# A graph layer on one core: the waits for products and for cleared places move from VectorE to TensorE

## Chip, cores and metric

The kernel runs on one core of one Trainium2 chip. The metric is the device time in microseconds (us) of one execution. The engines are named as the profile does: PE is TensorE's matmul, PEld its weight load, DVE VectorE, ACT ScalarE, POOL GpSimd, SP SyncE.

## The reference

x has 50,000 rows (nodes) of 256, and there are 25,000 edges, sorted by their destination `dst`. The parts that matter:

```
msg = relu(relu(layernorm(x))[src] + edge_attr)
p = msg @ W_fc.T + b_fc                      # one row of 256 per edge
scores = p @ Q.T                             # 4 heads
alpha = softmax of scores over the edges of one node, per head
pooled = segment_sum(alpha[:, h] * p, dst)   # per node, per head
gate = softmax(mean of p over the node's edges @ Wg.T + bg)
out = x + sigmoid(sum over h of gate[n, h] * pooled[n, h])
```

Since `gate` and `alpha` are numbers, each edge has one weight in the end, and the result of a node is the sigmoid of a weighted sum of its edges' rows `p`, added to x.

## The kernel before

**Edge stage.** The edges stand in 196 tiles of 128 rows. For each tile the x rows are gathered, normalized, added to the edge rows, transposed and multiplied, and the product p is kept in SBUF (`p_keep`, 124 tiles and 8 more places). 64 tiles are spilled to memory and reloaded later by SP, which raises `p_ready` as the tiles are there. In this stage a table is made as well: for each step of the node stage the address of its tile in `p_keep` and the place of its node tile in PSUM (`path`, twelve words per six steps), and per six steps one word that says how many tiles of p and how many cleared groups it needs (`needs_of`, in the tile `few`).

**Weights.** A stage of small operations, mostly on DVE, makes the weight of each edge.

**Node stage.** The 50,000 nodes are 391 tiles of 128, in 98 groups of four. A step pairs one tile of edges with one tile of nodes that it touches; there are 586. For each step DVE makes `spread` (L1248), a 128x128 matrix that holds an edge's weight in the column of its node, and PE multiplies it with the tile of p and adds the result in PSUM at the node tile's place (L829; in 32-bit floats the matrix makes two passes of it, so a step is two MATMUL and two LDWEIGHTS in the profile). PSUM has twelve places, three slots of a group each. When a group's steps are done (`stepped`), ACT takes the sigmoid of it (L597) and clears the slot (L573), which raises `zeroed`; POOL adds x (L478), and ACT issues the store (L605) and the next load of x (L552, every fourth by POOL at L482). A group is 512 KB in and 512 KB out.

**Order of the node stage.** It runs in turns of twelve steps, two half turns of six each; after the first turn both PE and DVE are in a loop (L836 and its like on DVE). The tile `spread` has twelve slots, and DVE's `spreads` waits for `stepped`, which starts at twelve, so it may make the spreads of six steps when PE has finished the six that used the same slots. In the half turn PE reads its twelve words with one TENSOR_LOAD (L819), waits for `spread_ready` before the first and the fourth step, and issues six matmuls. DVE reads the word of `needs_of` with one TENSOR_LOAD (`need_word`, L1252), waits for `p_ready` (L1256) and for `zeroed` (L1257), then makes six spreads. So PE needs no waits of its own for p and for the cleared places: a spread is made only when both are there. Each such wait compares a semaphore with a register, and loads and register instructions are done by the engine's sequencer, in order.

Of the kernel before, what the change touches and what calls it, by code (L numbers as in the profile page):

```python
# [34 lines left out]
def gnn_layer(nc, x, src, dst, edge_attr, w_fc, b_fc, q_w, g_w, b_g, out):  # L35
# [7 lines left out]
    TILES = -(-E // P)  # L43
# [33 lines left out]
    GROUPS = -(-NODES // GROUP)  # L77
    STEPS = TILES + NODES - 1
    AHEAD = 12
    HALF = AHEAD // 2  # L80
    TURNS = STEPS // AHEAD
# [23 lines left out]
    with ExitStack() as ctx:  # L105
# [3 lines left out]
        def sem(name):  # L109
            return ctx.enter_context(nc.semaphore(name))  # L110
# [37 lines left out]
        needs_of, done_of, free_of = few[0:1, :], few[32:33, :], few[64:65, :]  # L148
# [120 lines left out]
        words_stored, words_in = sem("words_stored"), sem("words_in")  # L269
# [19 lines left out]
        p_ready, zeroed = sem("p_ready"), sem("zeroed")  # L289
# [376 lines left out]
        def _(pe):  # L666
            pe.wait_ge(const_set, 10)
            pe.wait_ge(src_f32, 1)
            for b in range(BLK):
                last = nc.tensor.transpose(bank[:, 6, b * P:(b + 1) * P], src_f[:, b, :], ident[:, :])  # L670
# [3 lines left out]
            for c in range(KD):  # L674
                for t in range(KT):
                    last = nc.tensor.transpose(bank[:, 7, c * T + t * P:c * T + (t + 1) * P],
                                               w_nat[:, t, c * P:(c + 1) * P], ident[:, :])
            last.then_inc(w_turned, 1)
            for t in range(KT):
                last = nc.tensor.transpose(bank[:, 5, t * K:(t + 1) * K], qg[:, t * P:(t + 1) * P],  # L680
                                           ident[0:K, 0:K])
# [3 lines left out]
            for c in range(KD + 1):  # L685
                for t in range(KT):
                    lhs = b_col[:, t:t + 1].broadcast_to([P, P]) if c == KD else w_nat[:, t, c * P:(c + 1) * P]
                    last = nc.tensor.matmul(bank[:, 4, c * K:(c + 1) * K], lhs, q_t[:, t, :],
                                            start=(t == 0), stop=(t == KT - 1))
# [84 lines left out]
            for k in range(K):  # L774
                for b in range(BLK):
                    last = nc.tensor.transpose(bank[:, k // 2, (k % 2) * TP + b * P:(k % 2) * TP + (b + 1) * P],
                                               logits[:, b * P:(b + 1) * P, k], ident[:, :])
# [31 lines left out]
            for n, o, cols in ((7, 2 * P, slice(0, P)), (6, 0, slice(P, STEPS))):  # L809
                for b in range(BLK):  # L810
                    last = nc.tensor.matmul(bank[:, n, o:o + cols.stop - cols.start], c_of(b), sel_1[:, b, cols],
                                            start=(b == 0), stop=(b == BLK - 1))
# [2 lines left out]
            places = bank[:, :, :].rearrange("p b n -> p (b n)")  # L815
            p_rows = p_keep[:, :, :].rearrange("p t d -> p (t d)")

            def steps(half, s0, k0, n, apart=3):
                _, words = nc.values_load_multi_w_load_instructions(  # L819
                    path_of[:, bass.ds(half * WORDS, WORDS)], engines=[mybir.EngineType.PE], min_val=0,  # L820
                    max_val=(RING + STAGE) * T, skip_runtime_bounds_check_because=bound_by_shape)
                for k in range(n):
                    if k % apart == 0:
                        pe.wait_ge(spread_ready, s0 + k0 + min(k + apart, n))
                    p_at = nc.s_assert_within(words[k], 0, (RING + STAGE - 1) * T,
                                              skip_runtime_bounds_check_because=bound_by_shape)
                    place = nc.s_assert_within(words[HALF + k], 0, (POS - 1) * T,
                                               skip_runtime_bounds_check_because=bound_by_shape)
                    nc.tensor.matmul(places[:, bass.ds(place, T)], spread[:, k0 + k, :], p_rows[:, bass.ds(p_at, T)],  # L829
                                     start=False, stop=True, skip_group_check=True).then_inc(stepped, 1)  # L830

            pe.wait_ge(words_in, 64)
            pe.sem_inc(stepped, AHEAD)
            steps(0, 0, 0, HALF, 1)
            steps(1, 0, HALF, HALF)
            with pe.Fori(1, TURNS) as turn:  # L836
                for h in range(2):
                    steps(2 * turn + h, turn * AHEAD, h * HALF, HALF)
            s0 = TURNS * AHEAD
            steps(2 * TURNS, s0, 0, HALF)  # L840
            steps(2 * TURNS + 1, s0, HALF, STEPS - s0 - HALF)

        @block.vector
        def _(dve):
            steps = [0]
# [398 lines left out]
            def spreads(s0, k0, n):  # L1245
                dve.wait_ge(stepped, s0 + k0 + n)
                for k in range(k0, k0 + n):
                    v.tensor_scalar(spread[:, k, :], bank[:, 7, P:2 * P], rel[:, bass.ds(s0 + k, 1)],  # L1248
                                    wgt[:, bass.ds(s0 + k, 1)], ALU.is_equal, ALU.mult).then_inc(spread_ready, 1)

            def need_word(n):
                return dve.value_load(needs_of[:, bass.ds(n, 1)], min_val=257, max_val=(1 << 15) - 1)  # L1252

            def need(n):
                word = need_word(n)
                dve.wait_ge(p_ready, word & 255)  # L1256
                dve.wait_ge(zeroed, word >> 8)  # L1257

            dve.wait_ge(words_in, 64)
            first, second = need_word(0), need_word(1)  # L1260
            dve.wait_ge(p_ready, first & 255)
            dve.wait_ge(zeroed, first >> 8)
            dve.wait_ge(wgt_summed, 1)
            then(v.tensor_copy(wgt[:, 0:P], bank[:, 7, 2 * P:3 * P]))
            dve.sem_inc(wgt_ready, 1)
            spreads(0, 0, HALF)
            dve.wait_ge(p_ready, second & 255)
            dve.wait_ge(zeroed, second >> 8)
            spreads(0, HALF, HALF)
            dve.wait_ge(wgt_summed, 2)  # L1270
            then(v.tensor_copy(wgt[:, P:STEPS], bank[:, 6, 0:STEPS - P]))
            with dve.Fori(1, TURNS) as turn:
                for h in range(2):
                    need(2 * turn + h)
                    spreads(turn * AHEAD, h * HALF, HALF)
            s0 = TURNS * AHEAD
            need(2 * TURNS)
            spreads(s0, 0, HALF)
            dve.wait_ge(p_ready, TILES)
            dve.wait_ge(zeroed, GROUPS)  # L1280
            spreads(s0, HALF, STEPS - s0 - HALF)

            slot = (FULL - 1) % 4
# [35 lines left out]
```

## Time and profile before

| | us |
|---|---|
| median of 3 runs | 739.03 (735.18 to 739.16) |
| profiled execution | 734.6 |
| its span | 732.9 |
| PE, PEld busy | 548.9, 434.1 |
| DVE busy | 487.6 |
| ACT, POOL busy | 383.3, 453.4 |
| node stage | about 401 to 724 |

Register, branch, semaphore and DMA-issuing instructions don't count as busy; in a view of one line they stand under the engine's name with a q (PEldq, DVEq, ACTq), with their own durations. The DMA share is the mean busy share of the core's 16 DMA engines; packets that overlap can bring it a little over 1. The granted clock was 0.946 of full speed in the mean over the span. The waits view says for how long an engine was idle and whose end released it; "issue" means that nothing in the profile released it, so that its own sequencer was late.

### The profile page before, as it was taken

The page shows a single profiled execution, that of the slowest core. Times are in us where ns is not written, and L with a number is a line of the kernel's source. Part 1 is how long each engine was busy: PE and PEld are TensorE (multiplying, and loading weights), DVE is VectorE, ACT ScalarE, POOL GpSimd, SP SyncE. Part 2 cuts the span into 40 slices and gives each one's busy share as a digit, 9 for nine tenths or more (in the row PEclk, how much of TensorE's full clock was granted, in tenths as well). Part 3 has the DMA queues.
Part 4 walks back from the last instruction along what each step waited for, and adds up shares of the span by engine and source line. Part 5 has one row for each costly group of instructions (what it writes and reads, how often), then busy time and mean ns, then how long its engine had stood idle before and what let it go on. Part 6 is the DMA issues. An engine that isn't in the chain of part 4 may idle for free.

```text
span 732.9 us, 12416 instructions
## 1 busy us (share of the span) xinstructions
PE 548.9 (75%) x2474; PEld 434.1 (59%) x2475; DVE 487.6 (67%) x1644; ACT 383.3 (52%) x661; POOL 453.4 (62%) x339
## 2 busy tenths in 40 slices
PE   2417988878779868879403998888888778877785
PEld 2205876666558656758202876776667566665564
DVE  4208678788879768769798766666565655555555
ACT  2105455656457545647211254666666666666674
POOL 7765565665560656550053366777877887778785
PEclk9999899999999999989855999999999999999999
DMA  7434455555553468775300799999999999999999
GB/s 223 131 93 134 147 173 174 165 174 154 174 170 114 129 224 271 237 234 191 115 0 1 247 355 383 314 307 329 357 319 329 325 327 339 325 337 336 341 333 332
DMA packets 137238, 171.53 MB, mean 234 GB/s; under 512 B 10096, under 2 KB 123784, under 8 KB 137202
## 3 DMA queue, kind: packets, MB, share of 16 engines
q10 hardware_dynamic: 91344, 90.23, 37.6%
q1 hardware_dynamic: 33010, 42.70, 18.6%
q0 software_dynamic: 12848, 38.20, 16.5%
q8 instruction: 12, 0.20, 0.1%
q14 instruction: 24, 0.20, 0.1%
HBM read 111.50 MB, written 59.60 MB: 233 GB/s over the span
## 4 chain that ended last, share of the span: by engine, by line
PE 52%; issue 12%; ACT 11%; DVE 10%; another core or an unknown queue 5%; ACTq 4%; DVEq 3%; POOL 2%; DMA 2%; POOLq 0%; SPq 0%
PE bank L745 24%; PE bank L829 18%; PE bank L735 7%; ACT arena L597 5%; DVE spread L1248 3%; ACT bank L573 3%; POOL arena L478 2%; ACTq L600 2%; DVEq L1252 1%; ACT arena L505 1%; ACTq L552 1%; ACTq L605 1%; ACT arena L497 1%; DMA p_keep<-p_spill 1%
## 5 line engine op out<-in xcount | busy, mean ns | idle before, releaser
L829 PE MATMUL bank<-p_keep,spread 128*128 x1172 | 274.1, 388 | 51.6 <-DVE spread L1248 46.7
L829 PEld LDWEIGHTS bank<-p_keep,spread 128*128 128x128 f32 x1172 | 219.0, 192 | 107.5 <-issue 79.8
L1248 DVE TENSOR_SCALAR spread<-bank,rel,wgt 128x128 f32<-128x128 f32 x586 | 195.8, 404 | 128.5 <-PE bank L829 72.8
L478 POOL TENSOR_TENSOR arena<-arena 128x1024 f32<-128x1024 f32 x96 | 224.9, 2352 | 73.1 <-ACT arena L597 72.7
L745 PE MATMUL bank<-w_all,arena 128*128 128x264 f32 (+1 forms) x784 | 228.0, 417 | 53.2 <-ACT arena L505 40.2
L745 PEld LDWEIGHTS bank<-w_all,arena 128*128 128x128 f32 (+1 forms) x784 | 143.7, 204 | 78.9 <-ACT arena L505 50.9
L597 ACT ACTIVATE arena<-bank 128x1024 f32<-128x1024 f32 x97 | 99.2, 1023 | 139.3 <-PE bank L829 120.3
L443 POOL DMA_INDIRECT p_keep<-in_x_dram,idx x124 | 120.8, 975 | 72.6 <-issue 31.5
L505 ACT ACTIVATE arena<-bank 128x256 f32<-128x256 f32 x196 | 73.6, 376 | 124.2 <-PE bank L735 71.0
L443 POOL DMA_INDIRECT arena<-in_x_dram,idx x72 | 70.1, 973 | 64.7 <-ACT arena L497 33.7
L573 ACT ACTIVATE bank<-zero 128x1024 f32<-128x1024 f32 x98 | 100.5, 1026 | 3.0
L735 PE MATMUL bank<-ident,arena 128*128 128x128 f32 x392 | 80.5, 289 | 24.4 <-DVE arena L1061 11.3
L735 PEld LDWEIGHTS bank<-ident,arena 128*128 128x128 f32 x392 | 56.8, 149 | 53.2 <-DVE arena L1061 13.5
L1061 DVE TENSOR_TENSOR arena<-arena 128x256 f32<-128x256 f32 x196 | 79.8, 408 | 6.7 <-issue 3.9
L497 ACT ACTIVATE arena<-p_keep,negmr,rstd 128x256 f32<-128x256 f32 x124 | 73.6, 594 | 20.3 <-issue 14.1
L1075 DVE TENSOR_TENSOR p_keep<-bank,bias 128x512 f32<-128x512 f32 x97 | 66.0, 680 | 0.0
L1073 DVE TENSOR_TENSOR logits<-bank,bias 128x16 f32<-128x16 f32 x97 | 16.5, 170 | 64.7 <-PE bank L745 34.6
L1055 DVE BATCH_NORM_STATS2 stats<-p_keep 128x6 f32<-128x256 f32 x124 | 51.7, 419 | 1.0 <-DMA p_keep<-in_x_dram,idx 0.6
L497 ACT ACTIVATE arena<-arena,negmr,rstd 128x256 f32<-128x256 f32 x72 | 42.7, 593 | 9.5 <-DVE negmr L1099 7.5
L1055 DVE BATCH_NORM_STATS2 stats<-arena 128x6 f32<-128x256 f32 x72 | 30.2, 419 | 0.0
L449 POOL TENSOR_SCALAR arena<-arena 128x1024 f32<-128x1024 f32 x1 | 3.9, 3852 | 42.5 <-DVEq L1183 42.5
L482 POOL DMA_DIRECT2D arena<-in_x_dram x24 | 18.6, 773 | 17.6 <-POOL arena L478 14.8
(202 smaller groups left out, 190.6 us busy)
## 6 DMA issues: line engine op xcount, KB each, us to landing
out_dram<-arena ACTq DMA_DIRECT2D x97, 512.0 KB, 4.5
arena<-in_x_dram ACTq DMA_DIRECT2D x73, 512.0 KB, 5.4
arena<-in_edge_attr_dram SPq DMA_DIRECT2D x48, 512.0 KB
arena<-in_x_dram POOLq DMA_DIRECT2D x24, 512.0 KB, 5.8
p_spill<-p_keep SPq DMA_DIRECT2D x16, 512.0 KB
p_keep<-p_spill SPq DMA_DIRECT2D x16, 512.0 KB, 5.8
p_keep<-in_x_dram,idx POOLq DMA_INDIRECT x124
arena<-in_x_dram,idx POOLq DMA_INDIRECT x72
```

The source lines that it names most:

```text
L443: pool.indirect_dma_start(out=x_row(t), out_offset=None, in_=x, in_offset=bass.IndirectOffsetOnAxis(ap=idx[0:rows_of(t), t:t + 1], axis=0) ...
L478: pool.tensor_tensor(yout[:, slot, :, :], yout[:, slot, :, :], xin[:, slot, :, :], ALU.add).then_inc(summed, 1)
L497: nc.scalar.activation(u[0:n, t % 4, :], x_row(t), ACT.Relu, bias=negmr[0:n, m:m + 1], scale=rstd[0:n, m:m + 1]).then_inc(ln_done, 1)
L505: nc.scalar.activation(msg_t[:, t % 4, :, 0:n], bank[:, TURNS_IN[t % len(TURNS_IN)], 0:D].rearrange("p (c e) -> p c e", c=KD)[:, :, 0:n], ...
L573: nc.scalar.activation(bank[:, 2 * z:2 * z + 2, :], zero[:, 0:1].unsqueeze(2).broadcast_to([P, 2, 512]), ACT.Copy).then_inc(zeroed, 1)
L597: nc.scalar.activation(yout[:, k % YS, :, :], places(k % SLOTS, GROUP), ACT.Sigmoid).then_inc(sig_done, 1)
L735: last = nc.tensor.transpose(bank[:, TURNS_IN[t % len(TURNS_IN)], c * P:c * P + n], u[0:n, t % 4, c * P:(c + 1) * P], ident[0:n, 0:n])
L745: last = nc.tensor.matmul(bank[0:n, 2 + t % 4, 0:NT], msg_t[:, t % 4, c, 0:n], w_all[:, c, :], start=(c == 0), stop=(c == KD - 1))
L829: nc.tensor.matmul(places[:, bass.ds(place, T)], spread[:, k0 + k, :], p_rows[:, bass.ds(p_at, T)], start=False, stop=True, skip_group_che ...
L1055: v.bn_stats(stats[0:n, m, :], x_row(t)).then_inc(stats_done, 1)
L1061: v.tensor_tensor(u[0:n, t % 4, :], u[0:n, t % 4, :], ea[0:n, t % BODY, :], ALU.add).then_inc(added, 1)
L1248: v.tensor_scalar(spread[:, k, :], bank[:, 7, P:2 * P], rel[:, bass.ds(s0 + k, 1)], wgt[:, bass.ds(s0 + k, 1)], ALU.is_equal, ALU.mult).th ...
```

## The change

The two waits for `p_ready` and `zeroed`, and the load of the word that they compare with, leave DVE and go to PE, where they stand after the load of the path words and before the six matmuls. DVE's spreads now wait for `stepped` alone. The last half turn waits for constants.

```
+            def held(half):
+                word = pe.value_load(needs_of[:, bass.ds(half, 1)], min_val=257, max_val=(1 << 15) - 1)
+                pe.wait_ge(p_ready, word & 255)
+                pe.wait_ge(zeroed, word >> 8)
+
+            def held_last():
+                pe.wait_ge(p_ready, TILES)
+                pe.wait_ge(zeroed, GROUPS)
+
-            def steps(half, s0, k0, n, apart=3):
+            def steps(half, s0, k0, n, apart=3, last=False):
                 _, words = nc.values_load_multi_w_load_instructions(
                     path_of[:, bass.ds(half * WORDS, WORDS)], engines=[mybir.EngineType.PE], min_val=0,
                     max_val=(RING + STAGE) * T, skip_runtime_bounds_check_because=bound_by_shape)
+                if last:
+                    held_last()
+                else:
+                    held(half)
                 for k in range(n):
...
-            def need(n):
-                word = need_word(n)
-                dve.wait_ge(p_ready, word & 255)
-                dve.wait_ge(zeroed, word >> 8)
-
-            dve.wait_ge(words_in, 64)
-            first, second = need_word(0), need_word(1)
-            dve.wait_ge(p_ready, first & 255)
-            dve.wait_ge(zeroed, first >> 8)
             dve.wait_ge(wgt_summed, 1)
             then(v.tensor_copy(wgt[:, 0:P], bank[:, 7, 2 * P:3 * P]))
             dve.sem_inc(wgt_ready, 1)
             spreads(0, 0, HALF)
-            dve.wait_ge(p_ready, second & 255)
-            dve.wait_ge(zeroed, second >> 8)
             spreads(0, HALF, HALF)
...
             with dve.Fori(1, TURNS) as turn:
                 for h in range(2):
-                    need(2 * turn + h)
                     spreads(turn * AHEAD, h * HALF, HALF)
             s0 = TURNS * AHEAD
-            need(2 * TURNS)
             spreads(s0, 0, HALF)
-            dve.wait_ge(p_ready, TILES)
-            dve.wait_ge(zeroed, GROUPS)
             spreads(s0, HALF, STEPS - s0 - HALF)
```

On PE, at the head of the first half turn in the loop, this stood before; `path` is the table of twelve words per half turn, ISA and REGISTER_ALU are register instructions:

```order
L819 TENSOR_LOAD path
L824 ISA
L829 ISA [waits spread_ready]
L829 MATMUL bank<-p_keep,spread 128x256
L829 ISA
```

And this stands there now (L828, L837 and L842 are the lines that were L819, L824 and L829; `few` is the tile of the words that say what is needed):

```order
L828 TENSOR_LOAD path
L819 ISA
L819 TENSOR_LOAD few
L819 ISA x2
L820 REGISTER_ALU
L821 REGISTER_ALU [waits p_ready]
L837 ISA [waits zeroed]
L842 ISA [waits spread_ready]
L842 MATMUL bank<-p_keep,spread 128x256
L842 ISA
```

Between the load of the path words and the first matmul there are a second load, three ISA and two REGISTER_ALU instructions more, and the waits for `p_ready` and `zeroed`. The second half turn of the loop has the same.

On DVE, at the head of its loop, before:

```order
L1252 TENSOR_LOAD few
L1252 ISA x2
L1256 REGISTER_ALU
L1257 REGISTER_ALU [waits p_ready]
L1246 ISA [waits zeroed]
L1248 ISA [waits stepped]
L1248 TENSOR_SCALAR spread<-bank,rel,wgt 128x128
```

And now (L1261 was L1248):

```order
L1261 ISA [waits stepped]
L1261 TENSOR_SCALAR spread<-bank,rel,wgt 128x128
L1261 ISA
L1261 TENSOR_SCALAR spread<-bank,rel,wgt 128x128
L1261 ISA
L1261 TENSOR_SCALAR spread<-bank,rel,wgt 128x128
```

The load, its two checks and the two waits are gone, and the six spreads follow one another as before, held by `stepped` alone.

## Rows read from the trace of the kernel before

**Rows 1.** The page, parts 1 and 2: busy time, and the span in 40 slices
```profile
PE 548.9 (75%) x2474; PEld 434.1 (59%) x2475; DVE 487.6 (67%) x1644; ACT 383.3 (52%) x661; POOL 453.4 (62%) x339
...
PEclk9999899999999999989855999999999999999999
DMA  7434455555553468775300799999999999999999
GB/s 223 131 93 134 147 173 174 165 174 154 174 170 114 129 224 271 237 234 191 115 0 1 247 355 383 314 307 329 357 319 329 325 327 339 325 337 336 341 333 332
```

**Rows 2.** Busy time by stretches of the node stage (columns in the first row)
```profile
core 0: us, PE busy (x) PEld busy (x) DVE busy (x) ACT busy (x) POOL busy (x), PEclk, DMA share, GB/s
401.00:419.00 18.00, 18.00 (x85) 15.62 (x84) 14.61 (x44) 4.10 (x4) 4.37 (x3) 1.00 0.63 207
419.00:431.00 12.00, 11.41 (x53) 9.61 (x52) 8.58 (x26) 6.15 (x6) 6.81 (x4) 1.00 0.99 324
431.00:528.00 97.00, 85.71 (x374) 69.13 (x374) 61.60 (x185) 57.27 (x56) 72.23 (x36) 1.00 1.01 341
528.00:724.00 196.00, 156.32 (x654) 122.29 (x653) 109.65 (x328) 127.48 (x125) 157.70 (x79) 0.98 1.02 334
...
470.00:489.00 19.00, 17.59 (x81) 14.83 (x80) 12.10 (x37) 11.47 (x12) 13.53 (x8) 1.00 0.89 282
```

**Rows 3.** The waits from 401 to 729 us, longest first
```profile
engine line waited for: us in total, times, longest us
ACT arena L597 <- PE bank L829: 120.3, 74, 23.9
PEld bank L829 <- issue: 79.4, 72, 3.1
...
DVE spread L1248 <- ACT bank L573: 49.9, 27, 4.5
PE bank L829 <- DVE spread L1248: 46.7, 50, 2.7
```

**Rows 4.** Loads of L819, by stretches: 400-419, 470-489, 419-729, 401-431, 431-528, 528-724
```profile
engine op xcount: duration ns min/median/max, first and last start us, forms
...
L819 PEldq TENSOR_LOAD <-path x7: 848/857/865, 401.3 to 416.8; - x7
...
L819 PEldq TENSOR_LOAD <-path x7: 847/1130/1599, 470.2 to 485.7; - x7
...
L819 PEldq TENSOR_LOAD <-path x90: 846/1749/3016, 419.8 to 722.7; - x90
...
L819 PEldq TENSOR_LOAD <-path x11: 846/858/2638, 401.3 to 427.4; - x11
...
L819 PEldq TENSOR_LOAD <-path x32: 847/1586/2643, 431.6 to 528.0; - x32
...
L819 PEldq TENSOR_LOAD <-path x55: 847/1813/3016, 528.0 to 722.7; - x55
```

**Rows 5.** Loads of L819: from 634 to 639 us, then from 634 to 640.5
```profile
L819 PEldq TENSOR_LOAD <-path x2: 1294/1630/1965, 634.1 to 637.3; - x2
...
L819 PEldq TENSOR_LOAD <-path x3: 1294/1965/2268, 634.1 to 640.1; - x3
```

**Rows 6.** The chain of waits around one register load of ACT (L600)
```profile
642.41 0.03 issue
642.44 0.05 ACTq L600
642.49 0.03 issue
642.52 0.75 ACTq L600
643.27 0.03 issue
643.30 0.15 ACTq L600
643.45 0.03 issue
643.48 0.02 ACTq L600
643.50 0.04 issue
643.54 0.04 ACTq L596
643.58 0.04 issue
643.62 1.03 ACT arena L597
```

**Rows 7.** One-word loads: DVE (L1252) 400-419, 470-489, 419-729; then ACT (L600) 419-729
```profile
L1252 DVEq TENSOR_LOAD <-few x7: 301/310/316, 403.8 to 418.1; - x7
...
L1252 DVEq TENSOR_LOAD <-few x7: 301/315/979, 469.8 to 488.7; - x7
...
L1252 DVEq TENSOR_LOAD <-few x88: 300/578/1474, 420.4 to 717.3; - x88
...
L600 ACTq TENSOR_LOAD <-few x32: 279/766/1646, 423.1 to 724.2; - x32
```

**Rows 8.** Timeline, 396 to 401 us: the start of the node stage
```profile
396.91 4.20 PE L811 MATMUL bank<-logits,arena 128*128 128x128 f32 x8 [19.60 <-DVEq L1243]
...
398.65 0.29 DVE L1264 COPY wgt<-bank 128x128 f32<-128x128 f32 x1 [1.95 <-PE bank L811]
398.66 0.34 PEld L811 LDWEIGHTS bank<-logits,arena 128*128 128x128 f32 x1 [0.43 <-issue]
399.11 2.00 DVE L1248 TENSOR_SCALAR spread<-bank,rel,wgt 128x128 f32<-128x128 f32 x6 [0.16 <-DVE wgt L1264]
```

More of the change, by code:

```diff
@@ L840, in _ @@
             steps(2 * TURNS, s0, 0, HALF)
-            steps(2 * TURNS + 1, s0, HALF, STEPS - s0 - HALF)
+            steps(2 * TURNS + 1, s0, HALF, STEPS - s0 - HALF, last=True)
         @block.vector
@@ L1249, in spreads @@
                                     wgt[:, bass.ds(s0 + k, 1)], ALU.is_equal, ALU.mult).then_inc(spread_ready, 1)
-            def need_word(n):
-                return dve.value_load(needs_of[:, bass.ds(n, 1)], min_val=257, max_val=(1 << 15) - 1)
-            def need(n):
-                word = need_word(n)
-                dve.wait_ge(p_ready, word & 255)
-                dve.wait_ge(zeroed, word >> 8)
-            dve.wait_ge(words_in, 64)
-            first, second = need_word(0), need_word(1)
-            dve.wait_ge(p_ready, first & 255)
-            dve.wait_ge(zeroed, first >> 8)
             dve.wait_ge(wgt_summed, 1)
```

## Prediction, made before the changed kernel was run

> **What bounds the kernel now.** I read the page's parts 1 and 2 first, then the busy time by stretches, the waits of the node stage, and last the instructions of PE's own sequencer. The change touches only the node stage, from about 401 us to 724 us, so everything before it stays.
>
> The page shows the DMA digit at 9 from the middle of the span on, with 325 to 341 GB/s late in it [rows 1]. By stretches the DMA engines are at a share of 0.63 at the start of the stage, then at 0.99 to 1.02 to its end, while PE's matmuls are busy 86 of 97 us and 156 of 196 us [rows 2]. So two things are near their limit: the transfers (512 KB of x in and 512 KB of result out for each group) and PE.
>
> The waits [rows 3] show what the change is aimed at: PE stood 46.7 us, in 50 places, for DVE's spreads (L1248), and DVE stood 49.9 us for ACT's clears (L573), since DVE holds back weights whose places are not cleared yet. But the longest idle of PE's weight loads (PEld) is another, 79.4 us in 72 places, ended by "issue": the matrix was idle and PE's sequencer had not yet come to the next step.
>
> What the sequencer does there is L819, the TENSOR_LOAD of twelve words of `path` into registers, once per half turn of six steps. It takes 0.857 us in the quiet start of the stage, 1.130 us from 470 to 489 us, where the DMA share is 0.89 [rows 2], and 1.749 us (median of 90, up to 3.016) over the rest [rows 4]. The rest of a half turn is in the trace too. From 634.1 us three path loads start, the last at 640.1; the first two took 1.294 and 1.965 us [rows 5]. So two half turns took 6.0 us, of which 3.26 went on loads; 2.74 us, or 1.37 us per half turn, is everything else the sequencer issues for six steps. PE idled 0.6 us for a spread there at the beginning, while the sequencer was already past the load, so 1.37 holds little waiting.
>
> The sequencer's account per half turn is thus 1.37 + 1.75 = 3.12 us. The stage takes 323/98 = 3.30 us per half turn. PE's sequencer is occupied for about 95% of the node stage already; the matrix needs 12 passes in 2.6 to 2.7 us (the pace of the start, below). That is the point on which I put the prediction: the change adds work to an instruction stream with nearly no slack, to take a wait away.
>
> **The change part by part.** (a) DVE loses, per half turn, one TENSOR_LOAD of `few`, four register instructions and two waits. DVE is busy 110 of 196 us [rows 2], so this gives nothing by itself. Its spreads may now be up to twelve steps ahead, and the 46.7 us of PE's waits for spreads [rows 3] can go. What is late next is then PE's own wait for `zeroed`, which opens when ACT's clear is done, without the 0.4 us of a first spread (three of them, 1.2 us, before the first wait of a half turn) in between.
>
> (b) PE gains per half turn one TENSOR_LOAD of `few` and, by the order, three ISA and two REGISTER_ALU instructions and two waits, all ahead of its six matmuls; every LDWEIGHTS of the half turn is queued behind them, and ACT's sigmoid and DVE's reuse of the spread tiles wait for those. The register work: ACT does the same at L600. There 0.11 us passes from the earlier instruction's end to its load's start, and 0.31 us from 643.27, the load's end, to 643.58, with one ALU instruction; one more ALU with its gap is 0.07 [rows 6]. That makes 0.49, taken as 0.5 us.
>
> (c) The added load itself. The trace does not show PE loading one word. DVE's loads of the same tile take 0.310 us quiet, 0.315 at share 0.89 and 0.578 over the stage (up to 1.474), ACT's 0.766 [rows 7]. From below, nothing at all if it ran in the shadow of the path load; from above 1.5 us. On DVE two such loads and on PE load and next instruction follow one another, so I take it as serial and 0.65 us when the DMA engines are full, between DVE's median and ACT's.
>
> The Trainium skill, "DMA: Bandwidth & Descriptors", section "Latency and other measured facts", gives a floor of about 600 ns for such a load. The trace differs: 301 ns was measured [rows 7]. By the page's floor the quiet half turn below would be 0.3 us longer, an estimate, about 28 us over the stage.
>
> (d) Start and end of the stage: at the start PE is busy with L811 to beyond 399 us, DVE copies the weights at 398.65 after waiting 1.95 us for PE and spreads from 399.11 [rows 8]. DVE's two removed loads lay under that wait, PE's new one lies before the first spread is done. Zero; the cover is 1.95 us. The last half turn has constants instead of a load. Zero.
>
> (e) Sum. A half turn of PE's sequencer costs after the change:
> - quiet: 1.37 + 0.86 + 0.5 + 0.31 = 3.04 us
> - at DMA share 0.89: 1.37 + 1.13 + 0.5 + 0.32 = 3.32 us
> - at DMA share 1.01: 1.37 + 1.75 + 0.5 + 0.65 = 4.27 us
>
> The cost depends on how full the DMA engines are, and they get emptier if PE slows. So I look for the pace at which both agree, with a straight line between the last two (0.079 us per 0.01 of share). The path loads started [rows 4] give 11 half turns from 401 to 431, 31 to 528 (the one at 528.0 is in two rows) and 55 to 724.
> - 401 to 431: 2.73 us now, where PE's matrix is the bound. After: 3.06, since the engines are half empty. +0.33 x 11 = +3.6 us.
> - 431 to 528: 3.13 us now at share 1.01. At 3.48 us the share is 0.91 and the line gives 3.48. +0.35 x 31 = +10.9 us.
> - 528 to 724: 3.56 us now at 1.02. At 3.81 us the share is 0.95 and the line gives 3.81. +0.25 x 55 = +13.8 us.
>
> Together +28 us. Medians hide the long loads (0.979 and 1.599 among seven at share 0.89), for which I add 0.08 us per half turn, +8 us: +36 us. Against the profiled execution that is 734.6 + 36 = 771 us. The median of the three runs is 739.0, 4.4 us above that execution; the forecast is 775 us.
>
> Bounds: if the added load costs nothing beside the path load, the line lies at 3.00 and 3.62 us, and the same search gives about +8 us (747). If the loads stay as long as they are now although the transfers thin out, each half turn takes 4.27 us: 1.54 x 11 + 1.14 x 31 + 0.71 x 55 = +91 us, or +78 with the quiet figure kept in the first stretch (817).
>
> **The rivals.**
> 1. *The transfers stay the bound and nothing shows.* For it: share 1.01 and the quiet sequence of 3.04 us is below the 3.30 us of the stage; the loads stand ahead of the wait for `zeroed`, so they lie beside it. Against: it needs loads that are short while the DMA engines are full, and rows 4 and 7 say the contrary. 739 us, within 1%.
> 2. *It works as described (the other side).* PE's wait goes from the end of DVE's three spreads to the end of ACT's clear. If the whole added sequence cost under about 0.1 us per half turn beyond what it hides, a part of the 46.7 us would come back, as far as the DMA engines allow: their share is at 1.0, though one slice of the page reaches 383 GB/s, while tiles are reloaded, against 332 to 341 at the end [rows 1]. Taking 30% of the wait, -14 us: 725 us. It decides from the point where the added load and register work fit in the 3.30 - 3.12 = 0.18 us of slack, and they are 0.8 us at the least.
> 3. *Full price.* The loads are as long as before because it is each store or load burst that hits them and not the mean share; +78 us: 817 us.
>
> The Trainium skill, "Runtime: NRT & Kernel Launch", section "Instruction fetch mechanics", says that such loads cost about 200 ns per register. The trace disagrees: twelve words in 0.857 us are 71 ns each. By that rule the path load alone would take 2.4 us (an estimate) and the added one 0.2, which would make the change cheaper than by my rows, 0.7 us per half turn.
>
> **How the numbers follow.** The forecast (PE's sequencer becomes the bound, loads between their quiet and their full price, 750 to 800) has 0.66. Rival 3 (800 and more) has 0.14, rival 1 and the cheap end near 747 together 0.15, rival 2 0.05. A difference of 1%, 7 us, is about what a measurement tells from no change. Slower by over 1%: 0.66 + 0.14 and a part of the cheap end that is still over 7 us, 0.03, so 0.83; within 1% 0.12; faster 0.05. The range leaves out 1 in 10 on each side: 745 to 812 us.
>
> **What would show it.** In the profile after, waits of PE's matmuls for DVE spreads (46.7 us) should nearly vanish and PEld's idle ended by issue rise from 79 to over 140 us. Loads of `path` should have a median near 1.4 us, those of `few` on PE 0.4 to 0.5. The DMA share from 528 us on should fall to about 0.95 and the matrix's passes stand in groups of 12 with a gap before each. ACT's wait for PE (120.3 us) grows by about the whole loss. I am wrong if the DMA share stays at 1.0, if two loads on PE overlap, or if the granted clock, 0.98 to 1.00 in the stage, falls because of the gaps; this last would add to the loss.

## The result

The changed kernel takes 771.78 us in the median of 4 runs (769.07 to 775.86), the kernel before 739.1 (735.18 to 740.42): a ratio of 1.0456, interval 1.0394 to 1.0518. It is slower by 33 us; the forecast was 775, range 745 to 812.

The page of the changed kernel's profiled execution (770.83 us):

```profile
span 769.2 us, 12415 instructions
...
PE 556.7 (72%) x2474; PEld 433.8 (56%) x2475; DVE 487.1 (63%) x1643; ACT 383.6 (50%) x661; POOL 454.1 (59%) x339
```

The span grew by 36.3 us [rows 1 has the busy times of before], and no engine has more work: DVE 487.1 against 487.6, PE's matmuls 8 us more. The stretches of the node stage, to be held against [rows 2]:

```profile
core 0: us, PE busy (x) PEld busy (x) DVE busy (x) ACT busy (x) POOL busy (x), PEclk, DMA share, GB/s
401.00:419.00 18.00, 16.84 (x74) 13.74 (x73) 12.28 (x38) 2.92 (x3) 3.21 (x2) 0.97 0.57 183
419.00:431.00 12.00, 8.95 (x39) 6.95 (x38) 7.26 (x22) 3.23 (x4) 4.69 (x2) 1.00 0.78 259
431.00:545.00 114.00, 87.69 (x370) 67.44 (x368) 61.62 (x185) 59.02 (x58) 71.56 (x36) 1.00 0.90 289
545.00:760.00 215.00, 163.79 (x678) 126.73 (x679) 112.07 (x336) 130.07 (x128) 161.67 (x80) 0.98 0.97 311
```

The stage begins where it did (the first path load is at 396.6 us instead of 397.1) and its last path load is at 759.4 instead of 722.7. The DMA share was 0.99 to 1.02 from 419 us on; now it is 0.78, 0.90 and 0.97. So the transfers are no longer full all the time, and what holds them up keeps no engine busy. The waits, against [rows 3]:

```profile
ACT arena L597 <- PE bank L842: 172.5, 88, 24.7
...
PEld bank L842 <- issue: 117.8, 91, 3.0
...
PE bank L842 <- DVE spread L1261: 58.7, 49, 2.6
```

PE's weight loads (PEld) stood 117.8 us for "issue", 38 us more than before, and ACT stood 172.5 us for PE instead of 120.3. One row misleads. "PE waits for DVE spread, 58.7 us" seems to say that the change failed at its own aim. In order of time (start, length, engine, line, and in brackets the idle time before it):

```profile
646.71 2.01 DVE L1261 TENSOR_SCALAR spread<-bank,rel,wgt 128x128 f32<-128x128 f32 x6 [1.39 <-PE bank L842]
...
647.20 2.85 PE L842 MATMUL bank<-p_keep,spread 128*128 x12 [0.65 <-DVE spread L1261]
...
651.04 0.69 PE L842 MATMUL bank<-p_keep,spread 128*128 x2 [0.99 <-DVE spread L1261]
```

The six spreads that begin at 646.71 us are done at 648.72. The passes that use them begin at 651.04, 2.3 us later, and the view still puts the 0.99 us of idle down to the spread, since it is the last thing that a semaphore shows. The row "PE <- ACT bank L573", 16.6 us, which seems to name the wait for cleared places, misleads in the same way. What the sequencer did from 648.4 to 651.1 us stands in its own instructions:

```profile
L828 PEldq TENSOR_LOAD <-path x1: 1328/1328/1328, 648.5 to 648.5; - x1
...
L819 PEldq TENSOR_LOAD <-few x1: 306/306/306, 650.0 to 650.0; - x1
...
L819 PEldq SEQ_ASSERT  x1: 18/18/18, 650.6 to 650.6; - x1
...
L821 PEldq ALU_OP  x1: 36/36/36, 650.7 to 650.7; - x1
...
L837 PEldq FUSED_REGOPS  x1: 42/42/42, 650.8 to 650.8; - x1
```

The two loads, the check and the waits follow one another, and with the instructions that stand between these no gap is longer than about 0.06 us: the sequencer never stands still there. Counted like this over the trace (what a gap before an instruction that waits for a semaphore has beyond those 0.06 us), PE's sequencer stood 1.8 us in the whole stage before its semaphores, 0.3 us of it from 419 us on. Before the change it stood 34 us before `spread_ready`, in some 50 places (the expectation of e8_relay below has 31). The loads tell where the time is, first all from 419 us on, then those of three half turns (L828 the path words, L819 the word of what is needed; [rows 4, 5, 7]):

```profile
L828 PEldq TENSOR_LOAD <-path x91: 845/1232/2733, 419.6 to 759.4; - x91
...
L819 PEldq TENSOR_LOAD <-few x90: 299/306/1287, 421.1 to 757.6; - x90
...
L828 PEldq TENSOR_LOAD <-path x4: 846/1343/1467, 641.6 to 652.0; - x4
...
L819 PEldq TENSOR_LOAD <-few x3: 300/304/306, 642.6 to 650.0; - x3
```

From 641.6 to 652.0 us three half turns take 10.4 us. Their path loads took 0.85 us and twice about 1.34, their loads of `few` 0.91 together; the rest is 5.95, or 1.98 us per half turn, where it was 1.37 [rows 5]. Added up over the trace, the stage of 362.9 us holds 127.5 us of path loads (the last one begins at its end and is not in it), 38.2 us of the new loads, 1.8 us of waiting and 195.4 us of other instructions of PE's sequencer, 2.01 us per half turn. The stage before, 325.6 us, held 158.8 us of path loads, 34 us of waiting and 132.7 us of other instructions, 1.37 per half turn.

### The profile page after: what moved, and what is told of

It is laid out like the page before. It is cut to its first block, busy times and chain, and to the rows that moved or that the text cites. A ratio compares the mean times of both kernels' runs of the same rounds, so it can differ in the third digit from the quotient of the medians.

```text
span 769.2 us, 12415 instructions
## 1 busy us (share of the span) xinstructions
PE 556.7 (72%) x2474; PEld 433.8 (56%) x2475; DVE 487.1 (63%) x1643; ACT 383.6 (50%) x661; POOL 454.1 (59%) x339
## 4 chain that ended last, share of the span: by engine, by line
PE 59%; DVE 13%; issue 9%; another core or an unknown queue 6%; ACT 5%; DMA 3%; DVEq 1%; POOL 1%; ACTq 1%; POOLq 0%; SPq 0%
PE bank L842 30%; PE bank L745 21%; PE bank L735 6%; DVE spread L1261 4%; ACT arena L597 2%; ACT bank L573 1%; POOL arena L478 1%; DVEq L1261 1%; DVE stats L1068 1%; DVE p_keep L1088 1%; DMA p_keep<-in_x_dram,idx 1%; DMA p_keep<-p_spill 1%; DVE arena L1074 1%; ACT arena L505 1%
## 5 line engine op out<-in xcount | busy, mean ns | idle before, releaser
L842 PE MATMUL bank<-p_keep,spread 128*128 x1172 | 281.1, 391 | 81.7 <-DVE spread L1261 58.7
L842 PEld LDWEIGHTS bank<-p_keep,spread 128*128 128x128 f32 x1172 | 218.2, 192 | 145.4 <-issue 118.6
L1261 DVE TENSOR_SCALAR spread<-bank,rel,wgt 128x128 f32<-128x128 f32 x586 | 195.6, 403 | 164.7 <-PE bank L842 164.5
L597 ACT ACTIVATE arena<-bank 128x1024 f32<-128x1024 f32 x97 | 99.4, 1024 | 176.0 <-PE bank L842 172.5
L573 ACT ACTIVATE bank<-zero 128x1024 f32<-128x1024 f32 x98 | 100.5, 1026 | 3.0
L1074 DVE TENSOR_TENSOR arena<-arena 128x256 f32<-128x256 f32 x196 | 79.8, 408 | 10.9 <-ACT arena L497 7.0
```

Of the source, the lines that this page charges most:

```text
L573: nc.scalar.activation(bank[:, 2 * z:2 * z + 2, :], zero[:, 0:1].unsqueeze(2).broadcast_to([P, 2, 512]), ACT.Copy).then_inc(zeroed, 1)
L597: nc.scalar.activation(yout[:, k % YS, :, :], places(k % SLOTS, GROUP), ACT.Sigmoid).then_inc(sig_done, 1)
L1074: v.tensor_tensor(u[0:n, t % 4, :], u[0:n, t % 4, :], ea[0:n, t % BODY, :], ALU.add).then_inc(added, 1)
```

## The experiments

Theory S says that PE's sequencer sets the pace, by the instructions added to it. Rival W says that it is the waiting itself: PE alone holding the waits, or DVE running ahead. The experiments ran on several chips, and these differ in the edge stage: the kernel before took 657 to 658 us (median) on two of them and 731 to 739 on others. Every ratio is against the kernel before on the same chip, and where an expectation gives an absolute time, it was meant for the first chip. The node stage, from the first to the last path load, can be compared across chips: the changed kernel took 362.9 us in its first profile and 369.3 on a chip where the stage begins at 318 us (`after_again`), and the kernel before 325.6 in its first profile and 330.2 in `before_look`.

> The kernel before, one look, for the node stage's length beside e8_again. Its first profile had 325.6 us from the first to the last load of path words; if that doesn't depend on the chip, it is 322 to 330 us again, wherever the stage begins.

It came out at 330.2 us, the upper edge of that.

### Both engines wait (e1_both)

```
+ DVE: need(...) before each spreads(...), as in the kernel before; PE as in the changed kernel
```

> Both engines load the word and wait: PE as in the changed kernel, DVE as before. Theory S (PE's own instruction stream got longer, and it alone sets the pace): nothing is gained or lost against the changed kernel, 766 to 780 us. Rival W (it is DVE's running ahead, or PE alone holding the waits, that costs): with DVE held back as before the loss goes, 735 to 748 us.

701.11 us against 657.66, ratio 1.0692 (1.062 to 1.0763). With DVE held back exactly as before, the loss is all there. W's part on DVE's freedom falls. So does its part on the waits: in this run DVE has seen to both conditions before it makes the spreads, and PE's sequencer stood 0.4 us before `p_ready` and `zeroed` in the whole stage, counted as above.

### The changed kernel beside it (after_again)

> The changed kernel as it is, beside the kernel before on this chip, since the chips differ in the edge stage. Theory S: the node stage takes the 363 us of its first profile again, 33 to 37 us over the kernel before; both engines' waits (e1_both) and this one then differ by what DVE's freedom is worth.

697.25 us against 657.03, ratio 1.0578 (1.0523 to 1.0632), +40.2 us, a little more than expected; node stage 369.3 us and not 363. It differs from e1_both (+43.5 us) by 3 us, which the intervals don't separate (the two ran on different chips). So DVE's freedom alone is worth little while PE's stream is the bound.

### The load alone (e2_load_only)

```
+                extra = 0
+                if not last:
+                    _, (word,) = nc.values_load_multi_w_load_instructions(
+                        needs_of[:, bass.ds(half, 1)], engines=[mybir.EngineType.PE], ...)
+                    extra = word >> 15
...
-                    p_at = nc.s_assert_within(words[k], 0, ...
+                    p_at = nc.s_assert_within(words[k] + (extra if k == 0 else 0), 0, ...
...
```

> The kernel before, with one more one-word load of few on PE per half turn and no check and no wait (the word's upper bits, always zero, are added to the first step's address). Theory S: the load and its address instruction are 0.5 us of the about 1.0 us that the change added per half turn, and DVE's waits are still there as slack that takes a part; 745 to 760 us. Rival W: no wait has moved, so 737 to 742 us.

681.43 us against 657.66, ratio 1.0397 (1.0326 to 1.0468), +23.8 us, a little above what was expected. No wait was moved or added. Its wait row:

```profile
PEld bank L835 <- issue: 109.0, 96, 2.6
```

A load that nothing needs costs 60% of the whole loss, together with the instructions that address it and use its word (by the trace 0.38 us for the load and 0.28 for them, per half turn). The checks, the other ALU work and the waits are the other 16 to 20 us. The same row of e1_both:

```profile
PEld bank L842 <- issue: 130.1, 98, 2.8
```

### A third load (e4_third_load)

```
+                    _, (word,) = nc.values_load_multi_w_load_instructions(
+                        path_of[:, bass.ds(half * WORDS, 1)], engines=[mybir.EngineType.PE], ...)
+                    extra = word >> 17
                     held(half)
... (extra is added to the first step's address, as in e2_load_only)
```

> The changed kernel with a third load per half turn on PE (one word of path, unused but for zero bits). Theory S: 0.06 to 0.1 us of gap and 0.3 us of load more per half turn, partly given back as the DMA engines empty: +20 to +38 us on the changed kernel, 792 to 810 us. Rival W: a load that nothing waits for is hidden, 768 to 776 us.

729.24 us against 657.66, ratio 1.112 (1.1044 to 1.1197). That is 32 us over the changed kernel on a like chip (697.25), within what S expected and far from W's "hidden". The stretch from 420 to 650 us (columns as above), and the path loads and the third load:

```profile
420.00:650.00 230.00, 163.47 (x665) 125.90 (x664) 111.61 (x335) 123.02 (x120) 151.75 (x75) 0.97 0.87 273
...
L828 PEldq TENSOR_LOAD <-path x98: 850/958/2646, 317.1 to 718.8; - x98
...
L835 PEldq TENSOR_LOAD <-path x97: 305/307/1009, 318.2 to 716.5; - x97
```

The DMA share is down at 0.87, and the path loads, untouched, got shorter. Over five profiles with the words at the same places the mean path load gets shorter, by and large, as the stage gets longer: 1.64 us at a stage of 325.6 us, 1.48 at 350.4 (e2_load_only), 1.31 at 362.9 (the changed kernel), 1.34 at 372.7 (e1_both), 1.19 at 401.6 (e4_third_load). after_again has 1.39 at 369.3, before_look 1.59 at 330.2, e8_relay (below) 1.53 at 320.6.

### Thirteen words in one load (e3_thirteen)

The table that SP reads has the word of what is needed right behind the twelve path words, so one load can bring it.

```
-        path = sb("path", [P, HALVES, WORDS], I32)
+        path = sb("path", [P, HALVES, WORDS + 1], I32)
...
-                    path_of[:, bass.ds(half * WORDS, WORDS)], ...
+                    path_of[:, bass.ds(half * (WORDS + 1), WORDS + 1)], ...
...
-            def held(half):
-                word = pe.value_load(needs_of[:, bass.ds(half, 1)], ...)
+            def held(word):
+                word = nc.s_assert_within(word, 257, (1 << 15) - 1)
...
-                    held(half)
+                    held(words[WORDS])
```

> The changed kernel, but the word of what is needed comes as a thirteenth word with the twelve of the path, so PE has one TENSOR_LOAD per half turn; its check and both waits stay on PE. Theory S: about 0.5 of the added 1.0 us per half turn go, and the half turn costs PE's sequencer some 3.4 us when the DMA engines are nearly full: 740 to 756 us. Rival W: the waits are where they were, 766 to 776 us.

840.13 us against 657.66, ratio 1.2793 (1.2702 to 1.2885). Neither theory had that. The path loads:

```profile
L828 PEldq TENSOR_LOAD <-path x98: 1105/3576/7032, 317.7 to 826.4; - x98
```

They have a median of 3.6 us instead of 1.2, for one word more. So S was right on what sets the pace: the stage went to 508.7 us, 327 us of them path loads and under 1 us waiting. But nothing on record so far said what sets a load's length. Two theories: the number of words (N), or where they lie (A), since a half turn's words now start every 52 bytes and not every 48.

### Twelve words at 52 bytes (e7_stride13)

```
-        path = sb("path", [P, HALVES, WORDS], I32)
+        path = sb("path", [P, HALVES, WORDS + 1], I32)
...
+                    path_of[:, bass.ds(half * (WORDS + 1), WORDS)], ...
```

> The kernel before, still with twelve words per load, but the words of a half turn start at multiples of 52 bytes. Theory A: the loads get long as in e3_thirteen, the node stage goes to 450 us or more, +100 us. Theory N: the loads stay at 0.85 us at the least and 1.6 in the mean, and the time is that of the kernel before within 1%.

792.19 us against 657.03, ratio 1.2038 (1.1947 to 1.2129), in a kernel that differs from the one before in the distance of its words alone (SP copies thirteen words of each row, PE loads twelve). The expectation was +100 us, and it is +135. The loads of the quiet start in order, after the first, in three stretches (320 to 333, 333 to 335, 335 to 348 us):

```profile
L819 PEldq TENSOR_LOAD <-path x3: 2874/2876/2885, 321.3 to 329.4; - x3
...
L819 PEldq TENSOR_LOAD <-path x1: 854/854/854, 333.9 to 333.9; - x1
...
L819 PEldq TENSOR_LOAD <-path x3: 2867/2872/3716, 336.0 to 344.5; - x3
```

Three of 2.87 to 2.89 us, one of 0.854, then 2.87 twice and 3.72 (transfers had begun by then): every fourth is quick, and 4 x 52 = 208 is the first multiple of 52 that is one of 16. Theory A holds; N falls.

### Thirteen words at 64 bytes (e5_aligned)

```
-        path = sb("path", [P, HALVES, WORDS + 1], I32)
+        path = sb("path", [P, HALVES, 16], I32)
-        few = sb("few", [P, 2 * P], I32)
+        few = sb("few", [P, P], I32)
...
+                    path_of[:, bass.ds(half * 16, WORDS + 1)], ...
```

> The changed kernel with thirteen words per load again, but each half turn's words start at a multiple of 64 bytes instead of 52. Theory A (the long loads of e3_thirteen come from where the words lie): the load takes 0.9 us at the least and about 1.4 in the mean, the half turn some 3.4 us, 0 to +15 us against the kernel before. Theory N (they come from the number of words, thirteen instead of twelve): the load takes 3.4 us in the mean again and the run is +170 us or more.

682.29 us against 657.03, ratio 1.0365 (1.0323 to 1.0406), +25 us where theory A had 0 to +15:

```profile
L828 PEldq TENSOR_LOAD <-path x98: 1103/1583/4153, 317.1 to 672.3; - x98
```

The single load in place of two takes 15 us off the changed kernel (697.25 on the same chip), less than hoped: the shortest load is 1.103 us and not 0.9. The thirteenth word costs 0.26 us, as much as the one-word load's 0.30 that it was to save.

### The grain of a load (e9_stride14, e10_sixteen)

One word 0.30 us, twelve 0.846, thirteen 1.103, and twelve off the 16-byte places 2.87, thirteen 3.10: this fits 0.26 us per piece of 16 bytes when the words begin at a multiple of 16 bytes, and 0.24 us per word when they don't (theory G). Two kernels, each run once, test it:

> The kernel before, twelve words per load, a half turn's words at multiples of 56 bytes. Theory G (a register load takes about 0.26 us for each 16 bytes when it starts at a multiple of 16 bytes and about 0.24 us for each word otherwise): every second load is quick, 0.85 us in the quiet start, and the others take 2.87; the time lies between the kernel before and e7_stride13. Rival H (an 8-byte grain for starts at a multiple of 8): the others take about 1.5 us.

> e5_aligned with sixteen words per load instead of thirteen. Theory G: both are four pieces of 16 bytes, so the shortest load is 1.10 us in both and the times are equal within 1%. Rival (each word has its price): 1.10 + 3 x 0.05 = 1.25 us or, at the price of the thirteenth word, 1.9 us.

Twelve words at 56 bytes, five loads in the quiet start:

```profile
L819 PEldq TENSOR_LOAD <-path x5: 848/2887/2895, 397.2 to 409.9; - x5
```

They alternate, 2.89, 0.86, 2.89, 0.85, 2.90: starts at a multiple of 8 are as slow as others. The run took 816.02 us against 731.12. Sixteen words at 64 bytes:

```profile
L828 PEldq TENSOR_LOAD <-path x98: 1102/1572/3693, 394.1 to 747.3; - x98
```

1.102 us at the least, as with thirteen; 758.89 us against 731.12, a ratio of 1.038, as e5_aligned's 1.0365. Both came out as theory G says, and both rivals fall.

### Spreads ahead, the load left on DVE (e8_relay, e8_again)

```
-            def steps(half, s0, k0, n, apart=3):
+            def steps(half, s0, k0, n, apart=6):
...
-                    need(2 * turn + h)
                     spreads(turn * AHEAD, h * HALF, HALF)
+                    need(2 * turn + h)
+                    dve.sem_inc(released, 1)
...
                 for k in range(n):
+                    if k == 0:
+                        pe.wait_ge(released, half + 1)
```

With `apart=6` PE also waits for all six spreads of a half turn at once, and not for three and three. That part was not run by itself.

> The kernel before, with DVE making its six spreads first and then waiting for p_ready and zeroed, after which it raises a semaphore of its own (released), for which PE waits with a constant or the loop's count. So the spreads are ahead as in the change, and the load and checks stay on DVE. Theory S: PE's stream keeps its one load and grows by one wait, 3.0 to 3.2 us per half turn, so the loss is gone and a part of the 31 us in which PE's sequencer stood before the spreads comes back as far as the DMA engines allow: -3 to -15 us against the kernel before. Rival W (running ahead is what costs): +20 us or more.

> The same kernel as e8_relay, in more rounds. Theory S and what e8_relay showed: 0.982 to 0.993 of the kernel before. Rival (the 1.3% was a matter of that chip's rounds): within 0.5%.

651.27 us against 657.03, ratio 0.9873 (0.9813 to 0.9933), and in eight runs on another chip 724.22 against 731.95, 0.99 (0.9865 to 0.9935). This version beats the kernel before by about 1%, a small difference but clear of the intervals, and the changed kernel by much more. It has what the change was after, at one wait on PE instead of a load, a check and two waits. Its stretches (420 to 528 and 528 to 709 us) and waits:

```profile
420.00:528.00 108.00, 93.92 (x411) 75.68 (x411) 68.79 (x207) 62.39 (x61) 77.62 (x39) 1.00 1.02 337
528.00:709.00 181.00, 150.58 (x646) 119.72 (x645) 106.80 (x320) 124.45 (x123) 153.50 (x77) 0.99 1.04 351
...
PEld bank L832 <- issue: 70.7, 69, 3.0
...
PE bank L832 <- DVE spread L1251: 22.0, 21, 1.8
...
PE bank L832 <- DVEq L1281: 19.7, 19, 2.6
```

The same of the kernel before (`before_look`, its last stretch to 722 us):

```profile
420.00:528.00 108.00, 94.23 (x408) 77.19 (x408) 66.73 (x200) 64.10 (x63) 77.27 (x39) 0.98 1.01 339
528.00:722.00 194.00, 154.74 (x639) 120.86 (x640) 108.29 (x326) 124.28 (x122) 155.20 (x77) 0.97 1.00 330
...
PEld bank L829 <- issue: 79.9, 70, 2.9
...
PE bank L829 <- DVE spread L1248: 45.0, 46, 2.5
```

The DMA share of the last stretch goes from 1.00 at 330 GB/s to 1.04 at 351, and PE waits 22.0 + 19.7 us for DVE instead of 45.0. The stage is 316.2 us long against 330.2 (the medians of the whole kernels are 8 us apart). Counted as above, PE's sequencer stands 27 us before its semaphores instead of 44, while the path loads (155 and 154 us) and the other instructions (1.38 and 1.37 us per half turn) are the same: the gain is less waiting. Of the 27 us, 22 are before `released`, which DVE raises behind six spreads and its two waits; which of them was the last each time was not separated. That the transfers set it fits the share of 1.04, but no run shows it.

## Why the prediction was right, and what in it was not

- **The bound.** The central step, that what is added to PE's sequencer adds to the pace, held. After the change it hardly waits at all, a load that nothing needs costs 23.8 us, and a third load 32. The account of 3.12 of 3.30 us, 95%, was too high: it set the median load from 419 us on against the mean pace of the whole stage. With the means of the whole stage it is 1.37 + 1.64 = 3.01 of 3.36 us, 90%, and 0.35 us of slack instead of 0.18. The forecast doesn't use the slack, since it compares the pace before as measured with the sequencer's account after; only rival 2 was weighed by it.
- **The balance.** Of the stage's +37.3 us, the new loads are +38.2 and the other instructions +62.7; 31 us came back since the path loads got shorter and 32 because the waits went. So the waits did go, as the change meant, and they paid for a third of what was added.
- **(a) DVE's part.** Worth nothing by itself, as said. That PE's wait for spreads "can go" is true of the sequencer (34 us to under 2), but the row that I named for it went up, to 58.7 us. I had not reckoned with how the view names a releaser. That PE's wait for `zeroed` would be late next was wrong: the sequencer stood 0.3 us before it in the whole stage, for its own instructions are later.
- **(b) Register work, 0.5 us.** Too small: the rest of a half turn went from 1.37 to about 2.0 us. The length of the instructions was about right; the gaps were not. I took the sequence from ACT, where 0.03 us pass between two such instructions [rows 6]; on PE it is 0.06, at each of the six that were added.
- **(c) The added load, 0.65 us full and 0.32 at a share of 0.89.** Too large: 0.306 us in the median and 0.39 in the mean (38.2 us in 97). It was serial, as I took it. Why it is lengthened less than the path load before it stays open. The errors of (b) and (c) nearly cancel, which is luck: 0.65 + 0.39 = 1.04 us per half turn in the mean, where I had 1.15 at full transfers and 0.82 at a share of 0.89.
- **(d) Start and end.** Nothing: the first path load was 0.5 us earlier, and from the last one to the end of the span it is 9.7 us, before 10.1.
- **(e) The sum.** By half turns (11, 31 and 54 of them) the differences are +8.3, +18.2 and +11.1 us; I had +3.6, +10.9 and +13.8, and 8 us for the long loads that medians hide. The first stretch was mis-sized most for its size: its pace is 3.51 us and not 3.06. Quiet half turns take 3.0 and 3.35 us in turn, 3.2 in the mean and not 3.04, by (b); the rest is longer loads. The second reached 3.70 us and not 3.48. The third came to 3.81 as predicted, but at a DMA share of 0.97 and not 0.95. So the sum of 36 us is nearer to what was measured than its terms are.
- **The relief.** That path loads get shorter as the DMA engines empty was the step from +78 to +28 us. They went from 1.64 to 1.31 us in the mean (I had said near 1.4 for the median; it is 1.23), and the five profiles above show the same.
- **The rivals.** Rival 1 (hidden under the transfers) fell with the DMA share, and rival 3 (full price, 817 us) with the shorter loads. Rival 2, that it works, fell for this form of the change. Its mechanism is real, and e8_relay shows what it is worth: 1.0% to 1.3%, 6 to 8 us, where I had put 14 us.
- **The rules of the Trainium skill.** The floor of 600 ns ("DMA: Bandwidth & Descriptors" of the Trainium skill, section "Latency and other measured facts") doesn't hold here: 299 ns on PE. The 200 ns per register ("Runtime: NRT & Kernel Launch" of the Trainium skill, section "Instruction fetch mechanics") are said there of registers loaded from HBM, while `path` and `few` lie in SBUF, so the prediction took the rule where it need not hold. The figure is far from the 71 ns of an aligned load but close to what e7_stride13 shows off the 16-byte places, 2.87/12 = 0.24 us.
- **PEld's idle by issue** was to rise over 140 us and rose to 117.8; ACT's wait was to grow by about the loss and grew by 52.

## What to carry to other kernels

Before a wait moves to another engine, add up that engine's sequencer per turn, loads and register instructions included: it counts as busy nowhere, yet it was 90% full here. A condition whose bound must be read from memory is best checked on an engine with slack, which then raises a semaphore that the critical engine compares with a constant or the loop's count. Lay the words of a register load at multiples of 16 bytes and count them in fours.

## What was not expected of the hardware

- A TENSOR_LOAD into PE's registers took 0.85 us for twelve words beginning at a multiple of 16 bytes and 2.87 us elsewhere, both in the quiet start; under transfers the latter reached 6.7 us. In e7_stride13 this is 135 us of run time for a table's padding. The clock cost that run next to nothing, since the passes had room: against e5_aligned, with the same instructions and a granted clock of 0.95 to 1.00 over its stretches, the node stage is 153.5 us longer. Its path loads are 158 us longer, its waits 4 us shorter, and the other instructions take 1.86 and 1.87 us per half turn.
- PE's sequencer leaves 0.058 us from a register load's end to its next instruction, in the median of 94 cases before the change and of 194 after it; ACT's leaves 0.029.
- Two chips run the same edge stage some 78 us apart, while the node stage of the changed kernel agrees within 7 us (362.9 and 369.3). The reason was not looked for.
